# The first cross attention of a Flamingo block: split fp32r products replaced by plain fp32 products, with the exponential reading PSUM

## The reference, cut to what matters

```python
# x: (4, 1024, 256), ctx: (4, 154, 256); 8 heads of 128
xn = layernorm(ctx) * gamma_media + beta_media
ln = layernorm(layernorm(x)) * gamma_lat + beta_lat
q  = ln @ Wq + bq                                # (4, 1024, 1024)
k, v = split(concat([xn, ln], axis=1) @ Wkv + bkv)   # (4, 1178, 1024) each
attn = softmax(q @ k.T * 128 ** -0.5)            # per head: 1024 x 1178
x = x + tanh(g_xattn[0]) * ((attn @ v) @ Wo + bo)
```

## Time and profile before

| What | Value |
|---|---|
| Median of 3 runs | 3698.07 us (3697.74 to 3703.7) |
| Profiled execution: its own time | 3702.21 us |
| Profiled execution: span of the core | 3700.5 us |
| Mean granted TensorE clock | 0.951 |
| TensorE busy | 3237.7 us, 87% of the span |
| VectorE busy | 2511.6 us, 68% |
| ScalarE busy | 1736.3 us, 47% |
| GpSimd busy | 617.7 us, 17% |
| DMA | 43.13 MB, mean 12 GB/s |

### The profile page before, as it was taken

One profiled execution on the slowest core, in us unless ns is written; L12 is line 12 of the kernel. 1 busy time (PEld: TensorE's weight loads), 2 busy tenths in 40 slices (PEclk: granted clock), 3 DMA queues, 4 the chain that ended last, 5 costly groups with the idle time before them and its releaser, 6 DMA issues. The chain is left out here.

```text
span 3700.5 us, 59440 instructions
## 1 busy us (share of the span) xinstructions
PE 3237.7 (87%) x19570; PEld 2862.3 (77%) x19570; DVE 2511.6 (68%) x4651; ACT 1736.3 (47%) x3190; POOL 617.7 (17%) x665
## 2 busy tenths in 40 slices
PE   4999899998999989999599999999999799993454
PEld 3999889998999989999466787878788688882333
DVE  5666766666666666666666767777776666668887
ACT  3555555555555555555333322232322466653454
POOL 3111111111111121110211111111110233320000
PEclk9999999999999999999799999999999799995677
DMA  3000000000000000000200100010000000000001
GB/s 83 7 11 13 6 13 12 13 6 13 13 6 13 12 12 7 11 1 1 49 0 0 23 0 23 0 23 0 1 0 0 19 1 0 0 0 23 0 0 46
DMA packets 79094, 43.13 MB, mean 12 GB/s; under 512 B 32031, under 2 KB 78168, under 8 KB 78936
## 3 DMA queue, kind: packets, MB, share of 16 engines
q1 hardware_dynamic: 78936, 41.12, 4.1%
HBM read 36.91 MB, written 4.19 MB: 11 GB/s over the span
## 5 line engine op out<-in xcount | busy, mean ns | idle before, releaser
L369 ACT ACTIVATE x_pth<-x_ps 128x512 fp32r<-128x512 f32 (+1 forms) x768 | 374.8, 526 | 265.3 <-PE x_ps L574 265.0
L462 DVE TENSOR_TENSOR x_ptl<-x_ps,x_pth 128x512 fp32r<-128x512 f32 (+1 forms) x768 | 435.6, 594 | 75.9 <-ACT x_pth L369 67.7
L374 ACT ACTIVATE x_p<-x_p,x_nmx 128x1178 f32<-128x1178 f32 x256 | 327.7, 1280 | 249.4 <-DVE x_p L479 249.4
L829 ACT ACTIVATE moe_sil<-moe_ps,moe_b 128x512 f32<-128x512 f32 x256 | 176.1, 688 | 553.2 <-PE moe_ps L988 544.9
L574 PE MATMUL x_ps<-ident,x_p 128*128 128x128 f32 x2560 | 371.2, 275 | 42.9 <-DVE x_ptl L462 42.9
L596 PE MATMUL x_ps<-x_pth,x_vh 128*128 128x256 f32 x1280 | 374.8, 293 | 1.6 <-DVE xres L498 1.6
L574 PEld LDWEIGHTS x_ps<-ident,x_p 128*128 128x128 f32 x2560 | 301.0, 141 | 93.1 <-DVE x_ptl L462 73.8
L596 PE MATMUL x_ps<-x_ptl,x_vh 128*128 128x256 f32 x1280 | 364.6, 285 | 0.0
L596 PE MATMUL x_ps<-x_pth,x_vl 128*128 128x256 f32 x1280 | 364.4, 285 | 0.0
L479 DVE TENSOR_SCALAR_CACHE_REDUCE x_p<-x_ps 128x1182 f32<-128x1182 f32 x256 | 354.4, 1384 | 9.6 <-PE x_ps L583 1.4
L939 DVE TENSOR_TENSOR moe_gf<-moe_sil,moe_ps 128x512 f32<-128x512 f32 x256 | 175.5, 686 | 174.2 <-ACT moe_sil L829 173.8
(11 more groups left out here) (361 smaller groups left out, 7908.0 us busy)
## 6 DMA issues: line engine op xcount, KB each, us to landing
x_wraw<-in_L_xattn_Wkv_dram SPq DMA_DIRECT2D x64, 128.0 KB, 2.3
xres<-in_x_dram SPq DMA_DIRECT2D x4, 1024.0 KB, 7.7
x_wraw<-in_L_xattn_Wq_dram SPq DMA_DIRECT2D x32, 128.0 KB, 2.3
x_wraw<-in_L_xattn_Wo_dram SPq DMA_DIRECT2D x32, 128.0 KB, 2.0
moe_w1r<-in_L_ffn_w_dram SPq DMA_DIRECT2D x8, 512.0 KB, 5.3
moe_w2r<-in_L_ffn_w_dram SPq DMA_DIRECT2D x4, 1024.0 KB, 8.7
out_dram<-xres SPq DMA_DIRECT2D x1, 4096.0 KB, 13.5
ffn_w<-in_L_ffn_w_dram SPq DMA_DIRECT2D x2, 1024.0 KB, 6.9
```

What stands on the lines that cost most here:

```text
L369: act.activation(pth[:, (v // 2) % 2, lo:hi, (v % 2) * P:(v % 2 + 1) * P], ps[:, TURN + (v + g) % 2, 0:(hi - lo) * P].rearrange("p (n t) - ...
L374: act.activation(p[:, w % 4, DUP:DUP + R_KV], p[:, w % 4, DUP:DUP + R_KV], ACT.Exp, bias=nmx[:, w % 2:w % 2 + 1], scale=-1.0, accum_out=su ...
L462: dve.tensor_tensor(ptl[dst], ps[:, TURN + (v + g) % 2, 0:(hi - lo) * P].rearrange("p (n t) -> p n t", t=P), pth[dst].bitcast(F32), ALU.su ...
L829: act.activation(dst[:, q % 2, :], ps[:, HID + q % 2, :], ACT.Silu, bias=bias).then_inc(silu_done, 1)
```

## The change

The stage is rewritten with plain fp32 operands. No operand is split: each product is one `matmul` call. The scores are cut at 512, 1024 and 1178 keys. VectorE makes only the negated maximum from PSUM (`tensor_reduce`), and ScalarE's exponential reads the scores from PSUM and writes p; the next scores wait for it (`exp_done`). A group of transposed probabilities is read once: group 0 by ScalarE, groups 1 and 2 by VectorE. The values of four heads are made at a time, in the layout in which they are used, so they are not turned; their bias is folded into the output bias. All weights are loaded whole at the start (4 DMAs of 1 MB). GpSimd has two memsets and nothing else. The loop runs over batches, with the 64 steps of a batch in it; the next head's jobs are dealt over a head's 8 steps by `planned`. The statistics are made for the context and the first batch's tokens first, for the others behind the first jobs.

```diff
@@ resample_stage
-        kvh, kvl = sb("kvh", [P, KT, R_KV], F32R), sb("kvl", [P, KT, R_KV], F32R)
-        kh, kl = sb("kh", [P, 2, R_KV], F32R), sb("kl", [P, 2, R_KV], F32R)
-        pth, ptl = sb("pth", [P, 2, R_BLK, 2 * P], F32R), sb("ptl", [P, 2, R_BLK, 2 * P], F32R)
...
+        kvT = sb("kvT", [P, KT, R_ROW])
+        wq, wk, wv = (sb(n, [P, KT, R_INNER]) for n in ("wq", "wk", "wv"))
+        wo = sb("wo", [P, R_HEADS, DIM])
+        kT, qT = sb("kT", [P, 2, R_KV]), sb("qT", [P, 2, SEQ])
+        v = sb("v", [P, 2, R_BLK, HALF * P])
+        pT = sb("pT", [P, 2, R_BLK, 2 * P])
...
+        TURN_LAG, PV_LAG, Y_LAG = 2, 4, 5
+        XJOBS = [("x", k, lo, hi) for lo, hi in CUT for k in range(KT)]
+        def kq(n):
+            return [("k", n, lo, hi) for lo, hi in CUT] + [("q", n, lo, hi) for lo, hi in CUT[:2]]
+        def vals(half, lo, hi):
+            return [("v", half, n, None) for n in range(lo, hi)]
+        MAKES = [kq(1), kq(2) + vals(1, 0, 4), kq(3) + vals(1, 4, 7), kq(4) + vals(1, 7, R_BLK), kq(5), kq(6), kq(7)]
+        ENTRY = [XJOBS[0:2], [], XJOBS[2:5], XJOBS[5:6] + kq(0)[0:2], kq(0)[2:5], vals(0, 0, 4), vals(0, 4, 7), vals(0, 7, R_BLK)]
...
+        def planned(b, w, after):
+            n, s = w // TPB, w % TPB
+            if n < R_HEADS - 1:
+                at, m = len(ENTRY_ALL) + sum(len(x) for x in MAKES[:n]), len(MAKES[n])
+                return [(b, at + i) for i in range(s * m // TPB, (s + 1) * m // TPB)]
+            at = sum(len(x) for x in ENTRY[:s])
+            return [(b + 1, at + i) for i in range(len(ENTRY[s]))] if after else []
@@ scalar
-                    act.activation(p[:, w % 4, DUP:DUP + R_KV], p[:, w % 4, DUP:DUP + R_KV], ACT.Exp, bias=nmx[:, w % 2:w % 2 + 1], scale=-1.0,
-                                   accum_out=sums[:, w:w + 1]).then_inc(exp_done, 1)
+                x = behind(w, TURN_LAG, 1, before)
+                if x is not None:
+                    act.wait_ge(turned, 3 * (STEPS * b + x) + 1 + TURN0)
+                    act.activation(turn_dst(x, 0), turn_src(x, 0), ACT.Copy).then_inc(a_kept, 1)
+                if w < STEPS:
+                    act.wait_ge(turned, 3 * (STEPS * b + w) - 9 + TURN0)
+                    act.wait_ge(max_made, STEPS * b + w + 1)
+                    act.activation(p[:, w % 4, 0:R_KV], scores[:, 0:R_KV], ACT.Exp, bias=nmx[:, w % 2:w % 2 + 1],
+                                   accum_out=sums[:, w % (2 * TPB):w % (2 * TPB) + 1]).then_inc(exp_done, 1)
+                u = behind(w, PV_LAG, 2, before)
+                if u is not None:
+                    act.wait_ge(pv_done, UNITS * b + u + 1)
+                    act.activation(o[:, :], ps[:, PV, 0:2 * P], ACT.Copy).then_inc(o_kept, 1)
@@ vector
-                    dve.tensor_scalar(p[:, w % 4, 0:3 * SN].rearrange("p (b c) -> p b c", c=SN), scores, -1.0, R_BIG, ALU.mult, ALU.min,
-                                      accum_out=nmx[:, w % 2:w % 2 + 1]).then_inc(s_read, 1)
+                if x is not None:
+                    keep(b, x, 1)
+                if w < STEPS:
+                    W = STEPS * b + w
+                    dve.wait_ge(s_done, W + 1)
+                    dve.tensor_reduce(nmx[:, w % 2:w % 2 + 1], scores[:, 0:R_KV], AX.X, ALU.max, negate=True).then_inc(max_made, 1)
+                if x is not None:
+                    keep(b, x, 2)
@@ tensor
+                    for k in range(KT):
+                        if kind == "v":
+                            last = pe.matmul(out, kvT[:, k, lo * P:(lo + 1) * P], wv[:, k, i * HALF * P:(i + 1) * HALF * P],
+                                             start=(k == 0), stop=(k == KT - 1))
+                        else:
+                            last = pe.matmul(out[:, 0:hi - lo], (wk if kind == "k" else wq)[:, k, i * P:(i + 1) * P], kvT[:, k, lo:hi],
+                                             start=(k == 0), stop=(k == KT - 1))
...
+            def score(b, w):
+                pe.wait_ge(exp_done, STEPS * b + w + EXP0)
+                for lo, hi in CUT:
+                    last = pe.matmul(scores[:, lo:hi], qT[:, n % 2, t * P:(t + 1) * P], kT[:, n % 2, lo:hi], start=True, stop=True)
+                last.then_inc(s_done, 1)
...
+                for c in range(R_BLK):
+                    last = pe.matmul(ps[:, PV, 0:2 * P], v[:, n // HALF, c, (n % HALF) * P:(n % HALF + 1) * P], pT[:, u % 2, c, :],
+                                     start=(c == 0), stop=(c == R_BLK - 1))
...
+            def step(b, w, before, after):
+                if w < STEPS:
+                    for j in planned(b, w, after):
+                        job(*j)
+                x = behind(w, TURN_LAG, 1, before)
+                if x is not None:
+                    turn(b, x, 0)
+                    turn(b, x, 1)
+                if w < STEPS:
+                    score(b, w)
+                if x is not None:
+                    turn(b, x, 2)
+                u = behind(w, PV_LAG, 2, before)
+                if u is not None:
+                    values(b, u)
+                u = behind(w, Y_LAG, 2, before)
+                if u is not None:
+                    project(b, u)
```

More of the change, by code:

```diff
@@ L381, in first, with root_of @@
-            def first(jobs):
-                for n, m in jobs:
-                    job(n, m)
-            run(act, first, step)
+            act.sem_inc(exp_done, EXP0)
+            def root_of(rows, n):
+                act.wait_ge(stats, n)
+                act.activation(root[:, rows], var[:, rows], ACT.Sqrt).then_inc(rooted, 1)
+            early, late = slice(0, EARLY), slice(EARLY, NST)
+            act.wait_ge(d_in, 16 * ND)
+            root_of(early, 1)
+            root_of(slice(XAT, EARLY), 2)
@@ L387, in _ @@
+            for m in range(len(ENTRY_ALL)):
+                job(0, m)
+            act.activation(bvb, bias[:, 2, :].unsqueeze(2).broadcast_to([P, R_HEADS, P]), ACT.Copy).then_inc(bv_spread, 1)
+            root_of(late, 3)
+            root_of(late, 4)
+            act.activation(tg[:, :], tg[:, :], ACT.Tanh).then_inc(tanhed, 1)
+            steps(act, step)
         @block.vector
@@ L465, in step, with keep @@
-            def step(w, b, it, blag, jobs, norm):
-                for n, m in jobs:
-                    job(n, m)
-                for n in norm:
-                    normalise(*n)
-                behind = blag is not None
-                v = w - LAG
-                if (behind or v >= 0) and v < STEPS:
-                    lows(it, v, (0, 1))
+            def keep(b, x, g):
+                dve.wait_ge(turned, 3 * (STEPS * b + x) + g + 1 + TURN0)
+                dve.tensor_copy(turn_dst(x, g), turn_src(x, g)).then_inc(d_kept, 1)
@@ L640 @@
+            last.then_inc(bo_done, 1)
+            steps(pe, step)
 EXPERTS, TOPK, EH = 64, 8, 64
```

613 lines of the change are left out of this document (209 added, 404 removed).

## The result

The changed kernel takes 3884.21 us (median of 4 runs, 3880.03 to 3886.41) against 3697.9 before: a ratio of 1.050 (95% interval 1.0481 to 1.0518), 186 us slower. Forecast were 3940 and +242. The profiled execution has a span of 3883.4 us.

The account below looks back on a forecast made before the run. TensorE was taken to bound the rewritten stage. Products +269 us, vanished waits -85 and the score chain +58 gave +242, so a median of 3940 us, range 3860 to 4040.

Parts of the forecast that it names:

- The bound: In the rewritten stage TensorE sets the time; splitting work on the other engines costs it only 5%.
- The price of the fp32 product: On TensorE, a plain fp32 product is two records: 0.89 us at 512 columns, 0.433 at 256, against 0.69 and 0.36 split.
- the lower end: 512-column records on TensorE at exactly 0.434 us, 0.012 less on 1856 records: -22 us.
- the stream: TensorE's work in a loop step: 6.17 us before, 7.28 after, 1864 us for 256 steps.
- the same corrections for the first head and the inputs: From the loop's 1864 us, 25.5 lie before the loop and about 6 of inputs are in it: 1844.
- The waits that go: TensorE's waits in the loop, 46.4 us for v's copy and 38.4 for VectorE's remainders, all go: -85 us.
- The score chain: Next scores wait for maximum and exponential, 3.3 us; uncovered behind odd steps with few or no jobs: +58 us, bounds 0 and 130.
- The rival in which each odd step loses 2 us: In the score circle, copies ahead of maximum or exponential cost 256 us in place of 58: 4138; chance 0.09.
- Group changes, tail: In the loop, 54 us for TensorE's changes of group and the tail, unchanged by the rewrite.
- The start: Before the first scores: about 69 us, as before; taken as 0, with ends -8 and +10.
- The sum again: Stage end: 69 + 1844 + 58 + 54 = 2025 us in place of 1783, +242.
- Its +269: In TensorE's loop, 1844 us of stream after the change against 1575 before, the turned v included: +269 us.

Follow-up runs that it names:

- the runs in three: The changed kernel with scores and values, values alone, or every product as three fp32r matmuls in place of one fp32: 3731.1, 3795.11 and 3645.7 us.

## Why the prediction was right, point by point

It had the sign, the mechanism and the place; the time came out 56 us lower, inside the range. In the waits two errors partly cancel.

- **The bound.** TensorE's stream sets the stage: shown by the runs in three, which move the time by 153, 89 and 239 us. The first two change nothing but the form of the products; the third also brings its weights in another way, and 8 us of its gain lie before the first scores.
- **The price of the fp32 product.** Two records at 0.216 for 256 columns, as forecast; 0.43 for 512, forecast as 0.446. This is the step that was mis-sized. The 0.43 stood in the trace of before. Within the group of logits that starts at 1853.06, the second and the fourth record have these starts, in narrower windows:

```profile
1853.54 0.59 PE L1025 MATMUL moe_ps<-moe_lnT,moe_rw 128*64 x1
...
1854.39 0.59 PE L1025 MATMUL moe_ps<-moe_lnT,moe_rw 128*64 x1
```

The first interval is 0.48 us and the other two are 0.43 (0.858 for both); the mean of all three, 0.446, took the longer first one in. The figure scaled from 256 columns, 2 x 0.217 = 0.434, was named as the lower end and was right. With it scores take 1.98 us a step, k and q 0.925, v 0.54, and the stream 7.13 in place of 7.28: after the same corrections for the first head and the inputs 1807 in place of 1844, so -37 of the 57 us by which the stage ended early. The 154-column record at 0.13 was forecast as 0.14.

- **The waits that go.** Not all 85 us went. The 46.4 for v did; of the 38.4 behind the transposes 10.7 are left, now for VectorE's plain copy behind the maximum. And 85 was too low a count: by the starts these waits were about 100 us.
- **The score chain.** Forecast 58 us; covering it by the order gave back 47, taking the exponential out of it 36. The length, 3.3 us forecast and 3.0 measured, was too long since VectorE starts 0.20 us behind the stream's end and not 0.32, and since from the exponential's end to the next scores it is 0.14 us and not the 0.29 of accumulator read and release. The forecast that the wait would show as 60 us, 1 us at a time, was wrong: TensorE's list has 27.7 in 64 times, and the weight loads' 40.7 in 61, with 19.3 more for VectorE's copy. The rival in which each odd step loses 2 us did not happen.
- **Group changes, tail.** The loop's 1901 us less 1807 leave 94 for these and the chain, forecast as 112. That this came so near is partly luck. Of the 139 us beside the stream of before the forecast took 85 as waits and carried 54 over as changes of group; by the starts about 100 were waits, and those went. In their place came waits that it did not have: 19 us for VectorE's copy and about 16 for the next batches' inputs.
- **The start.** First scores at 66.3 us, forecast 69: the first transposes came 12 us earlier as reckoned (25.38 in the trace of after, 37.48 before), and the 40 records of v took 17.2 us of the room.
- **The sum again:** -3 at the start, -37 in the stream, -18 in the rest are, but for 1 us of rounding, the 57 us of 2025 - 1968.
- **What the forecast did not weigh.** Its +269 compares whole streams, with the v that is no longer turned in it, and its chain and waits stand apart. The runs cut it otherwise: 239 for the form of the product, less 56 for the rest of the rewrite, the circle included.

A product of 512 columns takes 2 x 0.43 us at a full clock, four times 512 cycles of 2.4 GHz and 1% more. By the rule of four passes (the Trainium skill, FP8 and Floating Point Precision, TensorE Precision Notes) that is what it should be, and the trace agrees. The ratio to three fp32r matmuls is not 4/3 all the same, but 0.86 to 0.69 = 1.25 at 512 columns, 0.43 to 0.36 = 1.20 at 256, and 0.26 to 0.30, under 1, at 154. Each fp32r matmul takes more beside its columns: with one column a cycle of 2.4 GHz taken off, an estimate, 0.02 us of 0.234 at 512, 0.01 of 0.120 at 256 and 0.04 of about 0.10 at 154, where an fp32 record, with two cycles a column taken off, has 0.003 at all three. Why this is so no run shows.

## What to carry to other kernels

Price a plain fp32 product and its split in three by rows of the width in question. Here 512 columns cost 0.86 us against 0.69, 256 columns 0.43 against 0.36, and 154 columns 0.26 against 0.30: wide products are cheaper split as long as other engines can make the remainders for nothing, narrow ones are not. Take the starts of single records, and leave out the first interval of a group. Read TensorE's stalls from starts, or from the waits of its weight loads, and not from its matmuls' waits alone. Before giving a buffer a longer life (scores held until the exponential), list for each step what the waiting engine has to do meanwhile; 1 us uncovered in one step of four was 47 us here, and moving jobs cured it in one kernel and hurt in another. The largest step was neither: where one rounding is exact enough, one fp32r product in place of one fp32 was worth 719 us for scores and values and 877 for all, and in place of three 566 and 639.

## What was not expected of the hardware

- VectorE's maximum of a step's scores takes 1384 ns without writing them out (1178 columns) and 1384 with it (1182 columns): the copy costs nothing here.
- ScalarE's exponential of 1178 elements is not slower from PSUM: 1243 ns against 1280 and 1278 from SBUF (the kernel before, and the changed kernel with the scores copied out).
- A 154-column fp32r matmul takes about 0.10 us from start to start (0.11 in the jobs of the kernel with every product in three), not much less than the 0.13 of one of the two records of an fp32 product of that width, and nearly as much as the 0.12 of a 256-column one.
- The list of TensorE's waits shows too little for a stalled matmul queue: removing 27 us of shown waits gave 47 us. The weight loads' waits fell by 45 us in that run, and by 36 where 36 us were gained.
